# Column sums of batch 1's context: eight tiles added on GpSimd ahead of one pass of TensorE

## The reference

```
x = x + attention(layernorm(x)) @ Wo          # 32 query heads, 8 key/value heads, RoPE, causal
x = x + fake_quant(layernorm(x)) @ fake_quant(context)      # context is 2 x 1024 x 1024
x = x + fixed_point_linear(layernorm(x))      # Q8.8 integers, 1024 x 1024 weights and a bias

def fake_quant(x, scale, zp):
    q = clip(round(x / scale + zp), 0, 255)
    return (q - zp) * scale
```

## Time and profile before

| | us |
|---|---|
| median of 3 runs | 495.21 (494.41 to 498.25) |
| the profiled execution's own time | 493.96 |
| its span in the trace | 492.1 |
| TensorE busy | 456.7 (93%) |
| VectorE busy | 364.5 (74%) |
| ScalarE busy | 300.0 (61%) |
| GpSimd busy | 285.5 (58%) |

### The profile page before, as it was taken

How to read it: one execution, slowest core, us unless ns; L and a number is a source line. 1 busy time by engine, 2 the same in 40 slices (tenths; PEclk the granted TensorE clock), 3 DMA queues, 4 the chain that set the end, 5 groups by cost and what they waited for, 6 DMA issues and landing times.

```text
span 492.1 us, 9896 instructions
## 1 busy us (share of the span) xinstructions
PE 456.7 (93%) x3986; PEld 259.9 (53%) x3986; DVE 364.5 (74%) x625; ACT 300.0 (61%) x302; POOL 285.5 (58%) x157
## 2 busy tenths in 40 slices
PE   0899999998999999999989999998889999999886
PEld 0775454554555565555545556555444444446542
DVE  5899766876777778777758777886475468799775
ACT  4684251316766876766858797789833412787632
POOL 5002651435899999999956877778820890607000
PEclk9999999998999999999989999999989999999999
DMA  8463595420321111111143202332266011000044
GB/s 343 160 240 108 180 287 156 179 75 23 125 83 55 33 40 52 46 55 55 35 150 109 82 35 103 110 107 102 73 217 254 24 41 43 1 1 2 1 173 173
DMA packets 21025, 50.84 MB, mean 103 GB/s; under 512 B 4848, under 2 KB 10096, under 8 KB 19696
## 3 DMA queue, kind: packets, MB, share of 16 engines
q1 hardware_dynamic: 19680, 41.70, 24.6%
q10 hardware_dynamic: 1296, 8.45, 4.9%
HBM read 40.57 MB, written 9.44 MB: 102 GB/s over the span
## 4 chain that ended last, share of the span: by engine, by line
PE 67%; DVE 16%; POOL 5%; ACT 5%; issue 3%; DMA 3%; SPq 0%; ACTq 0%; DVEq 0%; POOLq 0%
PE ps L1273 14%; PE ps L1451 12%; PE ps L1357 9%; PE ps L1338 7%; PE ps L1318 7%; PE ps L1586 5%; PE ps L1340 3%; PE ps L1320 3%; DVE stat L758 2%; PE ps L1541 2%; PE ps L1298 2%; DMA qstack<-in_x 2%; DVE mt L816 2%; ACT s1reg L558 1%; DVE wo_reg L1018 1%
## 5 line engine op out<-in xcount | busy, mean ns | idle before, releaser
L816 DVE TENSOR_REDUCE mt<-ps 128x1 f32<-128x512 f32 (+3 forms) x176 | 108.3, 636 | 32.0 <-PE ps L1320 31.6
L558 ACT ACTIVATE s1reg<-ps 128x1280 f32<-128x1280 f32 x64 | 78.8, 1232 | 55.7 <-PE ps L1340 55.7
L1273 PE MATMUL ps<-xT,wqx 128*128 128x512 f16 x384 | 95.3, 380 | 0.0
L1451 PE MATMUL ps<-wo_reg,xT 128*128 128x512 f16 x384 | 92.9, 378 | 2.4 <-POOL xT L1194 2.4
L1318 PE MATMUL ps<-kreg,qstack 96*128 96x512 f16 (+3 forms) x256 | 66.8, 304 | 3.9 <-DVE mt L816 1.8
L1338 PE MATMUL ps<-qstack,kreg 98*128 98x512 f16 (+3 forms) x256 | 58.2, 304 | 0.3 <-ACT s1reg L558 0.3
L1190 POOL TENSOR_TENSOR s1reg<-s1reg 128x1280 f16<-128x1280 f32 x19 | 49.7, 2623 | 12.2 <-ACT s1reg L564 12.2
L1451 PEld LDWEIGHTS ps<-wo_reg,xT 128*128 128x128 f16 x384 | 35.3, 97 | 37.1 <-POOL xT L1194 2.7
L1273 PEld LDWEIGHTS ps<-xT,wqx 128*128 128x128 f16 x384 | 35.0, 98 | 32.8 <-issue 0.3
L1190 POOL TENSOR_TENSOR wkv<-s1reg,wkv 128x1280 f16<-128x1280 f32 x18 | 47.2, 2630 | 8.8 <-ACT wkv L564 8.8
L1171 POOL TENSOR_TENSOR s1reg<-s1reg 128x512 f32<-128x512 f32 x11 | 16.0, 1450 | 60.5 <-DVE s1reg L807 60.5
(11 more groups left out here) (129 smaller groups left out, 963.1 us busy)
## 6 DMA issues: line engine op xcount, KB each, us to landing
s1reg<-in_weights ACTq DMA_DIRECT2D x8, 1024.0 KB, 5.3
s1reg<-in_ctx SPq DMA_DIRECT2D x16, 512.0 KB, 4.3
qstack<-rope_scratch SPq DMA_DIRECT2D x48, 128.0 KB, 2.6
rope_scratch<-s1reg SPq DMA_DIRECT2D x40, 128.0 KB, 2.2
qstack<-in_x SPq DMA_DIRECT2D x8, 512.0 KB, 5.6
s1reg<-in_x SPq DMA_DIRECT2D x16, 256.0 KB, 3.2
out<-s1reg SPq DMA_DIRECT2D x7, 512.0 KB, 2.7
s1reg<-in_L_ffn_weight SPq DMA_DIRECT2D x5, 512.0 KB, 5.9
```

Source lines behind the costliest of these rows:

```text
L558: nc.scalar.activation(ebuf[:, j % 2, :], st_ps[:, 0:SCORES], ACT.Exp, scale=EXP_SCALE, bias=P_LOG_SCALE).then_inc(e_done, 1)
L816: nc.vector.reduce_max(mt[:, G % 2, heads[0]:heads[-1] + 1, qt:qt + 1], ps[:, 3 + n % 2, 0:w * len(heads)].rearrange("p (h n) -> p h n", n ...
L1273: last = mm(out_ap, w(ws, k), xT[:, xs, KT * b + k, :], start=(k == 0 and n == 0), stop=(k == KT - 1 and n == 2))
L1451: last = mm(ps[:, bank, :], xT[:, os, KT * b + k, t], wo_sb[:, ws, 4 * h:4 * h + 4, k, :], start=(k == 0 and n == 0), stop=(k == KT - 1 an ...
```

## The change

GpSimd adds the eight tiles of batch 1 elementwise into one float16 tile, `ctx_sum`, which takes the place of one of the rotary tables. The numbers are whole and small, so that the sums are exact. TensorE multiplies only this tile by the ones: 2 matmuls in place of 16, placed after `output_b1(10)` in place of before `q1t(0)`, into banks 1 and 2. GpSimd's seven additions stand ahead of `corrections(0)`: five, then `weight_int(0)` and `weight_int(1)`, then the two that need tiles 14 and 15. On VectorE `columns(1)` moves behind `q1_zero_point(1)`. `context(0)` waits for the first column sums alone. Batch 0's sums stay as they are.

```diff
+        ctx_sum = rope[:, 1, :].bitcast(F16)
...
+        def sum_banks(b):
+            return two_banks(1 if b else 4)
...
             def columns(b):
                 dve.wait_ge(cb_done, b + 1)
-                nc.vector.tensor_scalar(cbz[:, b, :], flat(two_banks(4)), qs[:, 15:16], qs[:, 17:18],
+                nc.vector.tensor_scalar(cbz[:, b, :], flat(sum_banks(b)), qs[:, 15:16], qs[:, 17:18],
                                         ALU.subtract, ALU.mult).then_inc(cb_out, 1)
...
             q1_zero_point(0)
-            columns(1)
             output_add(9)
             q1_zero_point(1)
+            columns(1)
             context_add(0)
...
-            corrections(0)
+            def sum_context(k):
+                pool.wait_ge(ctx_done, KT + k + 1)
+                if k > 1:
+                    pool.wait_ge(ctx_summed, k - 1)
+                nc.gpsimd.tensor_tensor(ctx_sum, q2[:, KT, :] if k == 1 else ctx_sum, q2[:, KT + k, :], ALU.add).then_inc(ctx_summed, 1)
+
+            for k in range(1, KT - 2):
+                sum_context(k)
             weight_int(0)
             weight_int(1)
+            sum_context(6)
+            sum_context(7)
+            corrections(0)
             weight_int(2)
...
             def column_sums(b):
-                pe.wait_ge(ctx_done, KT * (b + 1))
                 if b:
-                    pe.wait_ge(cb_out, b)
-                else:
-                    pe.wait_ge(s_max, UNITS * NG)
-                    pe.wait_ge(o_norm, NG)
+                    pe.wait_ge(ctx_summed, KT - 1)
+                    for h in range(2):
+                        last = mm(sum_banks(b)[:, h, :], ones_h[:, :], ctx_sum[:, 512 * h:512 * h + 512], start=True, stop=True)
+                    last.then_inc(cb_done, 1)
+                    return
+                pe.wait_ge(ctx_done, KT)
+                pe.wait_ge(s_max, UNITS * NG)
+                pe.wait_ge(o_norm, NG)
...
                 if t == 0:
-                    pe.wait_ge(cb_out, B)
+                    pe.wait_ge(cb_out, 1)
+                    pe.wait_ge(o_norm, NG)
...
             output_b1(9)
-            column_sums(1)
             q1t(0)
             output_b1(10)
+            column_sums(1)
             q1t(1)
```

More of the change, by code:

```diff
@@ L202, in build @@
         q1_sum, q1t_done, q1t_out = sem("q1_sum"), sem("q1t_done"), sem("q1t_out")
-        cb_done, cb_out = sem("cb_done"), sem("cb_out")
+        cb_done, cb_out, ctx_summed = sem("cb_done"), sem("cb_out"), sem("ctx_summed")
         xa_done, xa_prepared, xa_added = sem("xa_done"), sem("xa_prepared"), sem("xa_added")
@@ L1517, in column_sums @@
             def column_sums(b):
-                pe.wait_ge(ctx_done, KT * (b + 1))
                 if b:
-                    pe.wait_ge(cb_out, b)
-                else:
-                    pe.wait_ge(s_max, UNITS * NG)
-                    pe.wait_ge(o_norm, NG)
+                    pe.wait_ge(ctx_summed, KT - 1)
[6 more added lines that the diff above has]
+                pe.wait_ge(o_norm, NG)
                 for h in range(2):
                     for k in range(KT):
-                        last = mm(two_banks(4)[:, h, :], ones_h[:, :], q2[:, KT * b + k, 512 * h:512 * h + 512],
+                        last = mm(sum_banks(b)[:, h, :], ones_h[:, :], q2[:, k, 512 * h:512 * h + 512],
                                   start=(k == 0), stop=(k == KT - 1))
```

## The result

| | before | changed |
|---|---|---|
| median, us | 495.21 (494.41 to 498.25) | 504.28 (499.99 to 506.13) |
| ratio to before, 95% interval | | 1.0168 (1.0109 to 1.0228) |
| profiled execution, us | 493.96 | 506.13 |
| its span, us | 492.1 | 504.3 |
| GpSimd busy, us | 285.5 | 300.7 |

What follows compares the result with a forecast made beforehand. TensorE alone was taken to bound the kernel from 362.9 to 423.6 us. -3.45 + 0.43 + 8.9 + 1.7 = +7.6 us on 493.96 gave 501.6, said as 502.0; own range 498.5 to 506 us.

Steps and rivals of the forecast that it cites:

- TensorE's matmuls: Batch 1's column sum on TensorE: 16 matmuls (3.45 us) go, 2 (0.43 us) come, -3.02 us.
- An addition: One 1024-column float16 addition on GpSimd: 2.14 us, scaled from L1190; seven would end at about 383.0 us.
- The rival of cheap additions: Float16 additions on GpSimd take near 1.12 us, so the kernel needs 493 to 494.5 us; chance 0.10.
- VectorE's chain: VectorE's steps from context tile 14 to q1t(0) stand behind GpSimd's instructions; q1t(0) can start at about 385.8 us.
- the rule that I weighed: On VectorE's narrow chain: beside running GpSimd, every step but the reciprocal is blocked, L771 to L778 at four columns included.
- the first rival: On VectorE's chain only forms seen blocked are blocked: stall 6.7, sum +5.4, 499.4 to 500.5 us; chance 0.10.
- The stall: TensorE stands from output_b1(9)'s end at 376.88 until q1t(0) at 385.8: +8.9 us.
- The clock: Behind TensorE's stall a lower granted clock costs 1.7 us, as in an earlier pause; bounds 0 and twice that.
- What is moved: Work around output_b1(10) and context(0): moved steps and removed waits cost nothing; corrections(0) ready by 394, cover 3 us.
- The sum: All terms on TensorE's chain together: -3.45 + 0.43 + 8.9 + 1.7 = +7.6 us.
- The time: The whole kernel: 501.6 us on the profiled execution's base, said as 502.0, own range 498.5 to 506.
- The rival that ended faster: VectorE always takes the port first, so GpSimd's additions hide: gain 2.5, 491.5 to 492.7 us; chance 0.06.

Runs made afterwards that it cites:

- the order only: The changed kernel's order on TensorE, with all 16 matmuls and no additions on GpSimd; ratio 0.997 to the kernel before.
- the filled stall: The changed kernel with 40 matmuls of no use on TensorE ahead of q1t(0); ratio 1.013 to the kernel before.
- the placed version: The changed kernel with three additions between context tiles 14 and 15, four between corrections(0) and corrections(1), two matmuls behind context(2); 493.89 us, ratio 0.996; repeated, 0.995.

## Why the prediction was right, point by point

- *TensorE's matmuls*, -3.02 us: 3.45 to 0.43 us, as said.
- *An addition*, 2.14 us: 2.13. Scaling to 1024 columns was the right choice; float32's 2.36 would have been 1.5 us too much in seven. The rival of cheap additions (1.12 us) is out.
- *VectorE's chain*: 22.9 us from the stage's start to q1t(0), forecast 385.8 - 362.9, measured 389.47 - 366.57 = 22.9. GpSimd won the first meeting (L947 took 2.63 us). Of the steps of `variance` and `inverse` that met a running GpSimd instruction, all but the reciprocal were blocked, at four columns too: L767, L774, L775 and L777. L776 passed in the gap that an addition's wait for the one before leaves; L778 came behind the seventh addition, when GpSimd was idle. So the rule that I weighed holds here and the first rival, in which only the forms already seen are blocked, is out. The run with the order only, in which nothing blocks, shows what each meeting costs: there q1t(0) starts 14.62 us after the normalisation, here 23.04, 8.42 us later. Tile 14 lost 1.88 us, tile 15 1.73, L767 0.84, L774 0.35, L775 1.90 and L777 1.86; less the 0.15 us that `output_add(8)` no longer waits for TensorE, that is 8.41. L767 and L774 (1.19 us of it) stood behind the two weights, not behind additions.
- *The stall*: 8.9 forecast, 8.93 measured.
- *The clock*: mis-sized. I took 1.7 us from the one pause in the earlier trace rows; it was (1.04 - 0.45) + (7.61 - 5.18) = 3.0, near the upper bound of 3.4, and the filled stall confirms 3.0. In the pause of the earlier trace rows the lower clock met 3.1 us of work, here 5.8.
- *What is moved*: corrections(0) began at 392.92 and was over by 396.8, context(0) ended at 402.5: cover enough.
- *The sum*: +7.6 forecast. By the terms -3.02 + 8.93 + 3.02 = +8.9; measured in the tail +8.5. At output_add(15) the shift is still 8.9 (436.19 - 423.60 - 3.67). Behind it 0.3 us come back: the chain's steps near the end lie 12.27 us later (501.14 against 488.87) in place of 12.59. Two matmuls of the last stage took 0.43 us in place of 0.61, and a wait 0.93 in place of 1.02.
- *The time*: 502.0 forecast, 504.28 measured, in the range. On the median of 495.21 the forecast +7.6 would have been 502.8; I took a value between the two bases, so 0.8 us of the miss is that choice and 0.9 us the tail. The other 0.5 us are within what varies ahead of the stage. In the profiled executions that part differs by 3.67 us. At about 73 us the changed kernel was still 0.7 us ahead. TensorE then waited 3.47 us for a transfer of the rotated heads (qstack from rope_scratch) where it had waited 1.11, and the next 12 matmuls of L1288 took 5.00 us in place of 2.75, at a granted clock of 0.50; from there it was 4.35 us behind. In the repeat of the changed kernel that wait was 2.24 us and the 12 matmuls took 2.75. So this explains one profiled execution, not the median.

The rival that ended faster (additions that hide entirely) is not false as an idea: the placed version is that case, at the place where VectorE has nothing to lose.

## What to carry to other kernels

Idle time of GpSimd is free only as far as VectorE has no chain of dependent SBUF instructions to walk in it: a step of the chain can cost one whole GpSimd instruction. Here seven steps, from L767 to L778 with the square root between them, took 6.5 us in place of 1.6. Before filling a hole, list what VectorE does in it and which of that TensorE waits for; then place the long instructions between such chains with a wait of their own, and look again at the meeting points after every later change.

## What the runs showed of the hardware

- Not every VectorE instruction is held: in the same window the statistics (L762) kept 0.70 us each beside running additions, and so did instructions with one operand in PSUM (L850, 0.69 us, at 377.22, and L994, 1.34 us, at 374.27). The number of inputs in SBUF alone doesn't tell: L762 reads one tile from there and passed, L947 reads one too and was held.
- In the trace before, `variance` on a single column passed as well: L763 on 128x1 at 430.57 took 0.14 us, while L1225 ran on GpSimd from 429.00 to 431.68. On two and on four columns the same line was held. No run here tests the other steps on one column.
- The loss to the clock did not follow the length of the stall: 3.1 us behind 3.7 us, 2.2 behind 5.2, 1.9 behind 5.5, 3.0 behind 8.9. It follows how much of TensorE's new work falls before the clock is back. In the 8 us from q1t(0) on, the granted clock was 0.60, 0.74, 0.78 and 0.64 in the mean, in the same order, and 8 x (1 - clock) is 3.2, 2.1, 1.8 and 2.9 us: within 0.2 us of what was lost. In the changed kernel's long stall the clock was already down for half the time (0.75 in the mean from 380.54 to 389.47), where it costs nothing; in the stall of 3.7 us it had hardly fallen when the work began (0.94 from 384.33 to 388.07). So one pause is not a price for another, and half filling a stall may save nothing of the clock's part.
- A float16 addition of 1024 columns on GpSimd takes 2.13 us against 2.36 in float32: half the bytes save a tenth.
